# Leaving out the 197 constant bf16 products on TensorE of a two-layer hybrid transformer kernel

## The reference, cut to what matters

```python
x = x + attn_a(layernorm(x))     # 16 heads, 4 latent kv heads, causal
x = x + moe(layernorm(x))        # 2 of 8 LoRA experts over a shared SwiGLU
x = x + head_mixer(layernorm(x)) # per token, heads attend to heads
x = x + moe(layernorm(x))
x = x + gated_delta(layernorm(x))# conv, 6 heads, delta-rule recurrence
x = x + ffn(layernorm(x))        # gelu, 1024 hidden
x = x + attn_b(layernorm(x))     # 16 query heads on one kv head, causal
x = x + ffn(layernorm(x))
```

## Time and profile before

| | before |
|---|---|
| median of 3 runs | 1312.31 us (1311.45 to 1312.48) |
| profiled execution, device time | 1312.18 us |
| its span in the profile | 1310.4 us |
| TensorE (PE) busy | 1202.5 us, 92% of the span |
| VectorE (DVE) / ScalarE (ACT) / GpSimd (POOL) busy | 677.2 / 416.9 / 229.6 us |
| mean granted clock of TensorE | 0.983 |
| constant products | 197 |

### The profile page before, as it was taken

One profiled execution on the slowest core, in us unless ns is written; L12 is line 12 of the kernel. 1 busy time (PEld: TensorE's weight loads), 2 busy tenths in 40 slices (PEclk: granted clock), 3 DMA queues, 4 the chain that ended last, 5 costly groups with the idle time before them and its releaser, 6 DMA issues.

```text
span 1310.4 us, 17604 instructions
## 1 busy us (share of the span) xinstructions
PE 1202.5 (92%) x6865; PEld 916.2 (70%) x6865; DVE 677.2 (52%) x1661; ACT 416.9 (32%) x897; POOL 229.6 (18%) x133
## 2 busy tenths in 40 slices
PE   6889999999998989988787999999999989899888
PEld 5677675767866778667565776757678677786666
DVE  5753266664465456334634433666644655663351
ACT  3623021313222342433453431313133223424352
POOL 0000074560110210000000000836501102100000
PEclk9999999999999999989998999999999999998989
DMA  8200000000000000000000000000000000000000
GB/s 350 115 1 1 1 1 1 1 1 1 1 1 2 1 1 1 1 2 9 1 9 1 1 1 1 1 0 1 0 1 1 1 1 1 1 1 2 1 1 17
DMA packets 3570, 17.32 MB, mean 13 GB/s; under 512 B 288, under 2 KB 2464, under 8 KB 2976
## 3 DMA queue, kind: packets, MB, share of 16 engines
q1 hardware_dynamic: 2912, 14.12, 2.7%
q10 hardware_dynamic: 576, 2.08, 0.4%
HBM read 15.15 MB, written 1.05 MB: 12 GB/s over the span
## 4 chain that ended last, share of the span: by engine, by line
PE 70%; DVE 11%; issue 9%; ACT 6%; POOL 2%; DMA 0%; DVEq 0%; POOLq 0%; ACTq 0%
PE bank L684 66%; ACT scr L1278 3%; PE bank L701 2%; DVE XnT L1960 2%; DVE XnT L1962 1%; DVE scr L1552 1%; DVE stat L1544 1%; POOL rstd L2116 1%; DVE negmax L1634 1%; PE bank L802 1%; DVE X L1537 1%; PE bank L1089 1%; ACT scr L1256 1%; POOL fac L2116 1%; ACT XnT L1256 1%
## 5 line engine op out<-in xcount | busy, mean ns | idle before, releaser
L684 PE MATMUL bank<-pack,scr 128*128 128x512 f32 (+2 forms) x944 | 312.1, 483 | 8.5 <-ACT scr L1256 7.5
L684 PE MATMUL bank<-XnT,pack 128*128 128x256 f32 x1024 | 251.3, 385 | 11.9 <-ACT XnT L1256 7.1
L684 PEld LDWEIGHTS bank<-pack,scr 128*128 128x128 f32 x944 | 178.5, 193 | 114.9 <-issue 89.4
L684 PE MATMUL bank<-scr,pack 128*128 128x256 f32 x944 | 227.0, 380 | 1.3 <-DVE scr L1715 1.1
L684 PEld LDWEIGHTS bank<-XnT,pack 128*128 128x128 f32 x1024 | 191.7, 192 | 45.4 <-ACT XnT L1256 9.6
L684 PEld LDWEIGHTS bank<-scr,pack 128*128 128x128 f32 x944 | 178.1, 190 | 30.3 <-issue 4.4
L2138 POOL TENSOR_TENSOR scr<-scr 128x1024 f32<-128x1024 f32 x64 | 149.9, 2379 | 47.3 <-DVEq L1777 46.6
L2116 POOL TENSOR_TENSOR rstd<-veps,half 128x2 f32<-128x2 f32 x32 | 22.3, 698 | 750.2 <-DVE veps L1549 750.2
L1725 DVE TENSOR_TENSOR scr<-bank,scr 128x256 f32<-128x256 f32 x112 | 47.2, 423 | 149.5 <-ACT scr L1329 148.6
L1278 ACT ACTIVATE scr<-bank,negmax 128x256 f32<-128x256 f32 (+1 forms) x256 | 82.9, 445 | 92.5 <-DVE negmax L1634 92.5
L1329 ACT ACTIVATE scr<-bank 128x256 f32<-128x256 f32 x112 | 42.6, 384 | 210.5 <-PE bank L684 210.3
(11 more groups left out here) (178 smaller groups left out, 1384.9 us busy)
## 6 DMA issues: line engine op xcount, KB each, us to landing
pack<-pack_dram SPq DMA_DIRECT2D x1, 6152.0 KB, 17.5
pack<-pack_dram SPq DMA_DIRECT2D x1, 2180.0 KB, 29.6
pack<-pack_dram SPq DMA_DIRECT2D x1, 1595.0 KB, 23.5
X<-x SPq DMA_DIRECT2D x4, 256.0 KB, 16.9
pack<-pack_dram SPq DMA_DIRECT2D x1, 1024.0 KB, 20.3
pack<-pack_dram ACTq DMA_DIRECT2D x1, 975.5 KB, 6.3
pack<-pack_dram SPq DMA_DIRECT2D x1, 793.5 KB, 25.0
out_dram<-X SPq DMA_DIRECT2D x3, 256.0 KB, 2.1
```

The lines of the kernel that those rows point to most:

```text
L684: return pe.matmul(o, l, r, start=start, stop=stop, skip_group_check=True)
```

## The change

`warm` sets its count to zero. Every call stays where it is and issues nothing. All claims, waits, semaphores and the order of all other instructions are the same.

```diff
             def warm(o, n):
+                n = 0
 
                 for _ in range(n):
                     mm(o.rearrange("p (c t) -> p c t", c=BANK // P), identb[:, :], ones4, True)
```

## The result

The kernel became slower: 1323.13 us median of four runs (1322.63 to 1324.67), against 1312.39 us for before on the same chip (1311.45 to 1313.19). The ratio is 1.0084, 95% interval 1.0067 to 1.0102, so 10.8 us were lost where I had forecast 3 us gained. The profiled execution took 1322.63 us.

A forecast was written before the change was run, and what follows sets the result against it. TensorE, busy 92% of the span with the chain on it for 70%, was taken as the bound. 1312.18 - 22.8 saved + 20.2 for low clock = 1309.6 us, stated as 1309.3; range for 8 in 10, 1297 to 1323 us.

The forecast's parts named there:

- What is saved: Constant products on TensorE's path: 90 at 0.22 us and 16 in delta_level at 0.19 us, 22.8 us saved.
- Fillers delay nothing: The other 91 constant products stand in TensorE waits; without them the same release comes at the same time, saving nothing.
- What the clock takes back: TensorE's clock falls where work is removed: 58 us more at the lower level, costing 20.2 us.
- How long: Added low clock: norm_t waits 7 us, delta block 17, attention 22, short waits 12; together 58 us.
- What price: Cost per us of low clock: 0.39 outside attention (14.0 us), 0.28 in it (6.2 us).
- The 0.16 of the earlier trace: Low price per us from attention's 550.45 to 559.79 us and its twin: 1.61 us for 10.2 us low.
- the second: Clock stays low through thinned delta and attention stretches: 90 to 110 us at 0.34, so 1320 to 1326 us; chance 0.27.
- Its point of decision: Additional low clock from which the stays-low case decides: 22.8 / 0.34 = 67 us.
- Faster and slower: Chances for the whole kernel: faster by over 0.2% 0.41, slower 0.40, within 0.2% 0.19.
- The stretch of 433 to 455 us: Narrow delta products of sequence a: 5.5 us shorter if the clock held, 2 to 4 us less so if not.
- wrong in kind: Sign: clock falls as forecast yet kernel over 10 us slower, or clock holds and the 22.8 us do not appear.

The follow-up runs named there:

- e9: The kernel before with the 100 constant products of delta_u, delta_s, delta_v and delta_o doubled; 1331.71 us, ratio 1.0136.
- e3: The kernel before without the 24 constant products ahead of the first dW in delta_level; 1309.73 us, ratio 0.9975.
- e12: The changed kernel, all constant products left out, timed again beside the kernel before; 1322.28 us, ratio 1.0074.
- e2: The kernel before without the 100 constant products of delta_u, delta_s, delta_v and delta_o; 1319.36 us, ratio 1.0046.
- e7: The kernel before without the 50 constant products of delta_u, delta_s, delta_v and delta_o for sequences b and d; 1313.66 us, ratio 1.0000.
- e4: The kernel before with all 197 constant products kept but run on 32 x 32 of the array instead of 128 x 128; 1355.40 us, ratio 1.0314.
- e8: The kernel before without the 50 constant products of delta_u, delta_s, delta_v and delta_o for sequences a and c; 1312.60 us, ratio 0.9993.
- e6: The kernel before without the 2 x 13 constant products of norm_t; 1314.04 us, ratio 1.0024.
- e1: The kernel before without the 65 constant products that fill waits in lora_t, norm_t and one values; 1323.63 us, ratio 1.0065.

## Why the prediction was wrong

- **What is saved: right.** 22.8 us were forecast, at 0.22 us a product. e9 shows 0.21 to 0.24 with hardly any clock in it, and e3 the 3 us of delta_level. At equal low clock e12 is 1294 - 1270 = 24 us ahead, but that figure leans on the price of 0.43. One reading was off: not all of the constant products ahead of the wait for ScalarE at 439.5 were on the path, and 0.4 us of theirs was not saved, at each of the two places.
- **Fillers delay nothing: right.** The waits got longer and ended at the same time, against the rows above.
- **What the clock takes back: the step that failed.** The prediction wrote 58 us of additional low clock and 20.2 us for it. There were 80 us, and they cost 10.45 + 22.8 = 33.2 us (10.45 us is 1322.63 - 1312.18, the two profiled executions). It is a product of two terms that were both too small.
  - *How long.* The delta block of a and c: 17 us estimated, while the trace has 3.4 + 10.2 + 23.9 less the 3.4 of before, 34 us. Behind norm_t: 7 estimated, 13.6 measured. lora_t, delta_level and `values`: 12 estimated, 13.7 measured behind lora_t alone. Attention was the other way, 22 estimated, 14 measured (30.7 with the stretch of 6.8 us at 1218.8, less the 17 of the earlier trace rows). The 5 us left come from parts that hold none of these products, but for 7 in `values` at 685 us.
  - *What price.* I took 0.39 outside attention and 0.28 in it, 0.35 on average. Measured: 33.2 / 80 = 0.42 for the whole, with the forecast's own 22.8 us taken as saved; 0.40 in e2 and 0.34 in e7 in the same way; 5.0 / 14 = 0.36 in attention; 10.9 / 24 = 0.45 in the worst stretch. The slopes over the runs of one kernel lie between 0.18 (e4) and 0.48 (e7), with 0.42 for e12, and the three sets of before have 0.24, 0.18 and 0.33, so the price is not one number. The 0.16 of the earlier trace rows was a row in which TensorE waited for softmax.
  - The missing 13 us are 22 x 0.35 = 7.7 for the length and 80 x 0.07 = 5.6 for the price.
  - *Where.* In the delta block of a and c the forecast was a gain of 54 x 0.22 - 17 x 0.39 = 5.3 us; the two traces show a loss of 4.9. That is 10 of the 13 us. Behind norm_t 5.1 us were lost for 2.7 forecast, in the short waits 4 x 1.65 = 6.6 for 4.7; attention gained 2.9 for 1.7. With the 3.3 us of delta_level these make 10.4 us, the whole difference of the two profiled executions.
- **The rivals.** In kind it went the way of the second, which was put at 0.27: once fallen, the clock stayed low through most of the narrow products, at worst for 23.9 us in one piece. The time, 1323.1 us, lies in that case's 1320 to 1326, but partly by luck: it asked for 90 to 110 us of low clock at 0.34, and there were 80 at 0.42. Its point of decision, 67 us of low clock at 0.34, is 22.8 / 0.42 = 54 us at the measured price. Either error alone would have turned the sign: 58 us at 0.42 are 24 us, and 80 us at 0.35 are 28. The rule of the Trainium skill (TensorE: Matmul & The Clock Gate, Part 1) puts the penalty at half of the throttled time. For 80 us that is 40 us; measured were 33.2, about as far below it as above the 28 us of my price.
- **Chances and range.** 1323.13 lies 0.13 us outside 1297 to 1323. Faster and slower stood at 0.41 and 0.40; that was fair for the difference of two sums of some 20 us each, of which one was an estimate. The point forecast of a gain had no more behind it than those chances.
- **What the trace was to show.** The clock was to be 0.961 for the forecast and 0.94 or below for the second case; it is 0.953, between the two. The clock at half behind the waits of norm_t came as written. The stretch of 433 to 455 us was to be 5.5 us shorter with the clock held and 2 to 4 us if not; up to the turns of L1007 it is 0.3 us shorter (22.22 to 21.91 us) and its twin 3.3 us longer (22.23 to 25.52 us), so the effect there was underestimated from the start. I was to be wrong in kind if the clock fell as much as I said and the kernel was more than 10 us slower. It is 10.8 us slower and the clock fell further, so this sign points at the size of the clock's term, and not at a cause outside it.

## What to carry to other kernels

A constant product that stands in a wait of TensorE delayed nothing here and held off falls that cost 1.65 us and more each; look for such places before you take the products for waste. On the path each costs its 0.22 us at full clock, and must win that back. Of the 197, 24 were a loss (delta_level), the 65 fillers earned 8.5 us, and the 100 narrow ones earned 6 us together though neither half of them showed a gain alone. Falls move when something else changes, so an edit's total can hide its effect in place, as in e8: time it over many runs, and compare the edited stretch itself in the traces. When you price a low clock, take stretches where the chain runs over TensorE, here 0.40 to 0.45 us per us, and not the ones where it waits anyway.

## What the runs showed of the hardware that I had not expected

- Over 23.6 us TensorE was busy for 22.77 with the clock at half throughout; with the constant products on 32 x 32 of the array it was busy 29.67 of 30.50 us, and low too.
- fp32 products 64 columns wide slow down at the lower level nearly as much as wide ones (8 of them: 1.34 us to 2.4 us, 1.8 times; wide ones 1.97 times), so narrow work was no shelter from a low clock.
- After an edit, falls went or came in parts of the program that the edit leaves alone (e6 and e8 at 560.8 and 1202.5 us), and two executions of one program had them in different places (the changed kernel at 150, 307 and 687 us).
- One and the same program spread over 18 us (e1: 1311.35 to 1329.47), with mean clocks from 0.986 to 0.972. A single run of such a kernel says little; its time has to be read together with its clock.
